# A transformer sandwich layer on one core: output projection three tiles ahead of the mixture, and a last tile in another order

## The chip, the cores and the metric

The kernel runs on one core of a Trainium2 chip. The metric is the device time of one execution, in microseconds (us). The core has five engines with a program each: TensorE (PE in the profile; its weight loads are PEld), VectorE (DVE), ScalarE (ACT), GpSimd (POOL) and SyncE (SP), which issues the DMAs here. Each executes in the order of its own program; they meet only at semaphores.

## The reference

```python
x = x + layernorm(attention(layernorm(x)))      # x: 4 x 512 x 1024, float32
x = x + layernorm(mixture(layernorm(x)))

def attention(x):   # 16 heads of 64, rotary on q and k, causal softmax
    ...
    return out @ Wo                              # Wo: 1024 x 1024

def mixture(x):     # 8 experts of rank 16
    scores = 8 * softmax(x @ Wr.T + br)
    low = einsum('bsd,hrd->bshr', x, A)
    return 2 * einsum('bshr,hor,bsh->bso', low, B, scores)
```

Every float32 product is made of three: each factor is split into a high and a low part, and high x high, low x high and high x low are added in PSUM.

## The kernel before, in words

The first part (projections, rotary, attention per pair of heads) writes the attention output to a scratch tensor and isn't touched. The part that matters here runs over 16 token tiles of 128 tokens. A tile t passes through these steps (names as in the code):

- `y_half`: y(t) = oT(t) @ Wo, on PE: 8 chunks by 3 products by two halves of 512 columns, 48 matmuls, into the two banks `y_ps[i]`, i = t % 2.
- `y_variance`, `ln_scale`: the layernorm's statistics on DVE (`bn_stats`, `bn_aggr`), the reciprocal root on ACT (Ln, Exp) refined on DVE; then ACT writes z in two halves; DVE adds the input (`x1`); statistics again and ACT writes `xn2`, the normalised tile.
- `x2_turn`, k = 0 and 1: PE transposes xn2, four blocks at a time, into the single bank `tr_ps`; ACT copies the high part (`x2T_high`), DVE subtracts the low part (`x2T_lo`). Because there is one bank, k = 1 waits until both have read k = 0.
- `low_rank`: 24 matmuls of 136 columns into `o_ps` give low and the router's logits; DVE and ACT make the softmax and the weighted low (`wlow`).
- one transpose of wlow (`wlt_done`), high and low part by ACT and DVE (`wlT_hi`, `wlT_lo`), and `experts`: 6 matmuls of 512 columns into `pt_ps`.
- a third layernorm (its number is `ln_third`), res on ACT, the last addition on POOL, the store by SP.

All engines walk through `turn(t, i)`, t = 0 to 17: in turn t, y is made for tile t, the middle steps (`x2_turn`, `low_rank`) for tile t - 1, and `experts`, the third layernorm and the store for tile t - 2. PE's turn puts the pieces of the other tiles between parts of y(t): first 15 matmuls of y(t), the transpose of wlow, 9 more, experts, 12 more, `x2_turn` k = 0, 9 more, `x2_turn` k = 1, the last 3, `low_rank`. y(0) is made in the last slots of attention. ACT's turn has x2T_high of the middle tile at its start and xn2(t) at its end. In turn 0, after xn2(0), ACT and DVE also split the mixture's constants (`ar`, `bt`, lines 759, 760, 1013, 1015). Nothing but these written orders and the semaphores sets what runs when.

## Time and profile before

| | |
|---|---|
| median of 3 runs | 1184.49 us (1184.37 to 1185.08) |
| profiled execution | 1184.45 us, span from first to last instruction 1182.7 us |
| PE busy | 1089.5 us, 92% of the span |
| DVE, ACT, POOL busy | 756.7, 628.3, 438.3 us |
| mean granted TensorE clock | 0.970 of full speed |

Times in the rows count from the start of the span. In a timeline row the first number is the start, the second the duration (of the matmuls the modelled one, which overlaps the next; the distance of two starts is what one costs), and the bracket is how long the engine was idle before it and what ended the wait. A row without a bracket follows its predecessor without a wait worth telling.

### The profile page before, as it was taken

The page shows a single profiled execution, that of the slowest core. Times are in us where ns is not written, and L with a number is a line of the kernel's source. Part 1 is how long each engine was busy: PE and PEld are TensorE (multiplying, and loading weights), DVE is VectorE, ACT ScalarE, POOL GpSimd, SP SyncE. Part 2 cuts the span into 40 slices and gives each one's busy share as a digit, 9 for nine tenths or more (in the row PEclk, how much of TensorE's full clock was granted, in tenths as well). Part 3 has the DMA queues.
Part 4 walks back from the last instruction along what each step waited for, and adds up shares of the span by engine and source line. Part 5 has one row for each costly group of instructions (what it writes and reads, how often), then busy time and mean ns, then how long its engine had stood idle before and what let it go on. Part 6 is the DMA issues. An engine that isn't in the chain of part 4 may idle for free.

```text
span 1182.7 us, 20255 instructions
## 1 busy us (share of the span) xinstructions
PE 1089.5 (92%) x5616; PEld 905.7 (77%) x5616; DVE 756.7 (64%) x2075; ACT 628.3 (53%) x1435; POOL 438.3 (37%) x412
## 2 busy tenths in 40 slices
PE   2899999999999776899999999999976999999984
PEld 2688888888888664688888888888865888888873
DVE  7656666666666675666666666666664666666663
ACT  4445555555555545555555555555564454544542
POOL 3053543535435232153543535435253223323311
PEclk9999999999999988999999999999989999999995
DMA  5111101111012113011101101010424132333210
GB/s 213 54 36 33 63 13 62 44 31 62 14 61 82 43 59 98 5 50 28 62 24 51 49 27 62 27 48 14 134 63 140 57 104 95 101 106 106 84 40 36
DMA packets 37499, 73.44 MB, mean 62 GB/s; under 512 B 3152, under 2 KB 19536, under 8 KB 37456
## 3 DMA queue, kind: packets, MB, share of 16 engines
q1 hardware_dynamic: 37456, 72.92, 19.0%
q8 instruction: 20, 0.33, 0.1%
q14 instruction: 23, 0.19, 0.1%
HBM read 56.14 MB, written 16.78 MB: 62 GB/s over the span
## 4 chain that ended last, share of the span: by engine, by line
PE 78%; DVE 8%; ACT 6%; issue 6%; DMA 1%; POOL 1%; POOLq 0%; DVEq 0%; SPq 0%; ACTq 0%
PE bank L1076 40%; PE bank L1034 30%; PE bank L1103 5%; ACT prob L591 1%; PE bank L1055 1%; PE bank L1195 1%; DVE prob L833 1%; DVE big_lo L822 1%; ACT pT_hi L602 1%; DVE q_hl L865 1%; DVE stats L776 1%; DVE stats L777 1%; DVE rr L797 1%; ACT xn L561 1%; DMA w_raw<-in_wqkv 1%
## 5 line engine op out<-in xcount | busy, mean ns | idle before, releaser
L1076 PE MATMUL bank<-big_hi,w_hi 128*128 128x512 f32 x768 | 335.9, 437 | 16.1 <-DVE big_lo L822 13.4
L474 POOL TENSOR_SCALAR prob<-prob,rinv 128x128 f32<-128x128 f32 (+3 forms) x256 | 156.6, 612 | 508.6 <-DVE rinv L843 508.6
L591 ACT ACTIVATE prob<-prob,nmax 128x128 f32<-128x128 f32 (+3 forms) x256 | 143.6, 561 | 353.4 <-DVE nmax L833 352.1
L1076 PE MATMUL bank<-big_hi,w_lo 128*128 128x512 f32 x768 | 306.4, 399 | 0.0
L1076 PE MATMUL bank<-big_lo,w_hi 128*128 128x512 f32 x768 | 304.4, 396 | 0.0
L1076 PEld LDWEIGHTS bank<-big_hi,w_hi 128*128 128x128 f32 x768 | 147.5, 192 | 33.7 <-issue 17.5
L1076 PEld LDWEIGHTS bank<-big_hi,w_lo 128*128 128x128 f32 x768 | 146.2, 190 | 34.4
L851 DVE TENSOR_TENSOR pT_lo<-bank,pT_hi 128x128 fp32r<-128x128 f32 (+3 forms) x256 | 123.9, 484 | 57.4 <-ACT pT_hi L602 54.1
L1076 PEld LDWEIGHTS bank<-big_lo,w_hi 128*128 128x128 f32 x768 | 148.4, 193 | 12.0
L843 DVE RECIPROCAL rinv<-rsum 128x1 f32<-128x1 f32 x256 | 40.8, 160 | 159.2 <-ACT prob L591 159.1
L833 DVE CUSTOM_DVE_ANT_0 prob<-bank,mask 128x128 f32<-128x128 f32 (+3 forms) x256 | 124.3, 486 | 22.3 <-PE bank L1034 18.4
L1103 PE MATMUL bank<-ident,prob 128*128 128x128 f32 x640 | 113.3, 275 | 1.5 <-DVE pT_lo L851 1.5
L1034 PE MATMUL bank<-big_hi,w_hi 128*128 128x512 f32 x256 | 106.7, 417 | 7.7 <-POOL big_lo L516 5.2
L602 ACT ACTIVATE pT_hi<-bank 128x128 fp32r<-128x128 f32 (+3 forms) x256 | 108.7, 425 | 4.1 <-PE bank L1103 2.5
L1103 PEld LDWEIGHTS bank<-ident,prob 128*128 128x128 f32 x640 | 84.1, 142 | 31.8 <-issue 2.5
L1034 PE MATMUL bank<-big_lo,w_hi 128*128 128x512 f32 x256 | 101.6, 397 | 0.0
L1034 PE MATMUL bank<-big_hi,w_lo 128*128 128x512 f32 x256 | 101.0, 395 | 0.0
L492 POOL TENSOR_TENSOR w_lo<-w_sum,w_hi 128x1024 fp32r<-128x1024 f32 x32 | 85.7, 2679 | 11.7 <-ACT w_hi L584 11.7
L1034 PE MATMUL bank<-k_hh,q_hl 128*128 128x128 f32 (+3 forms) x256 | 83.1, 325 | 2.4 <-DVE k_hh L872 1.9
L1034 PE MATMUL bank<-k_lo,q_hl 128*128 128x128 f32 (+3 forms) x256 | 83.6, 326 | 0.0
L532 POOL TENSOR_TENSOR res<-res,x 128x1024 f32<-128x1024 f32 x16 | 38.3, 2396 | 120.3 <-ACT res L561 120.3
L1034 PE MATMUL bank<-pT_hi,v_hl 128*128 128x512 f32 (+3 forms) x256 | 76.6, 311 | 1.5 <-ACT pT_hi L602 1.5
(106 smaller groups left out, 1921.4 us busy)
## 6 DMA issues: line engine op xcount, KB each, us to landing
w_raw<-in_wqkv SPq DMA_DIRECT2D x48, 512.0 KB, 3.6
attention_out<-o_sum SPq DMA_DIRECT2D x64, 128.0 KB, 2.3
xin<-attention_out SPq DMA_DIRECT2D x16, 512.0 KB, 4.8
xres<-in_x SPq DMA_DIRECT2D x16, 512.0 KB, 3.5
out<-res SPq DMA_DIRECT2D x16, 512.0 KB, 2.6
xin<-in_x SPq DMA_DIRECT2D x14, 512.0 KB, 3.7
w_raw<-in_wo SPq DMA_DIRECT2D x6, 512.0 KB, 4.3
prob<-in_x SPq DMA_DIRECT2D x2, 512.0 KB, 7.7
```

Of the source, the lines that this page charges most:

```text
L474: pool.tensor_scalar(p, p, rinv[:, q % 4:q % 4 + 1], 1.0, ALU.mult, ALU.mult).then_inc(prob_done, 1)
L492: pool.tensor_tensor(w_lo[:, m, :], src, w_hi[:, m, :].bitcast(F32), ALU.subtract).then_inc(w_lo_done[m], 1)
L532: pool.tensor_tensor(res[:, i, :], res[:, i, :], x1[:, i, :], ALU.add).then_inc(res_done, 1)
L561: return act.activation(dst, src, ACT.Identity, bias=nmr[:, 0:1], scale=rstd[:, 0:1])
L591: act.activation(prob[:, q % 4, 0:n], prob[:, q % 4, 0:n], ACT.Exp, scale=-1.0, bias=nmax[:, q % 4:q % 4 + 1], accum_out=rsum[:, q % 4:q % ...
L602: act.activation(pT_hi[:, h, 0:i + 1, P * i:P * i + P], pt_ps[q % 2][:, 0:P * (i + 1)].rearrange("p (j t) -> p j t", j=i + 1), ACT.Copy).t ...
L833: dve.tensor_tensor_reduce(prob[:, q % 4, 0:n], sc_ps[q % 2][:, 0:n], mask[:, SEQ - n:SEQ], -SOFT, 3e38, ALU.add, ALU.min, nmax[:, q % 4:q ...
L843: dve.reciprocal(rinv[:, q % 4:q % 4 + 1], rsum[:, q % 4:q % 4 + 1]).then_inc(inv_done, 1)
L851: dve.tensor_tensor(pT_lo[at], pt_ps[q % 2][:, 0:P * (i + 1)].rearrange("p (j t) -> p j t", j=i + 1), pT_hi[at].bitcast(F32), ALU.subtract ...
L1034: mm = pe.matmul(dst, lhsT, rhs, start=first and n == 0, stop=last and n == len(terms) - 1)
L1076: done = pe.matmul(grp_ps[(b + k) % 2][:, :], w, xt, start=at == 0, stop=at == GROUP_MM - 1)
L1103: last = pe.transpose(pt_ps[q % 2][:, P * j:P * j + P], prob[:, q % 4, P * j:P * j + P], ident[:, :])
```

## The change

Everything behind `y_half` moves one turn later: in turn t the middle steps belong to tile t - 2, and experts, third layernorm and store to tile t - 3, so there are 19 turns (0 to 18). x1 gets four buffers and xn2 two, since they live longer. The turns run through a common `run_turns`, whose loop covers four turns at a time (turns 4 to 11); the last seven are written out. The numbers of the layernorms follow the new order.

In turn 15 (`last`), y(15) is not divided by `x2_turn`: its second half runs whole, and both `x2_turn`s of tile 13 and low_rank(13) come behind it. ACT and DVE have an order of their own there. In turn 18 the last res goes in two halves: ACT signals each, DVE (not POOL) adds each, and SP stores each. out_out starts at 16 so that its counts fit.

```diff
-        x1 = sb(sC, "x1", [P, 2, EMBED])
+        x1 = sb(sC, "x1", [P, 4, EMBED])
-        xn2 = sb(sC, "xn2", [P, EMBED])
+        xn2 = sb(sC, "xn2", [P, 2, EMBED])
+        last_done = sem("last_done")
...
-            return TILES + 3 * t - 1 if late(t, 2) else TILES + 2 * t
+            return TILES + 3 * t - 2 if late(t, 2) else TILES + 2 * t
...
-            return 4 * TILES - 1 if isinstance(t, int) and t == TILES - 1 else TILES + 3 * t + 4
+            return 2 * TILES + TILES + t if isinstance(t, int) and t >= TILES - 3 else TILES + 3 * t + 6
+        def run_turns(eng, turn):
+            for t in range(4):
+                turn(t, t)
+            with eng.Fori(4, TILES - 7, 4) as t:
+                for j in range(4):
+                    turn(t + j, j)
+            for t in range(TILES - 4, TILES + 3):
+                turn(t, t % 4)
...
+                sp.sem_inc(out_out[h], 16)
...
-                if tiled(t - 2):
-                    sp.wait_ge(res_done, t - 1)
-                    sp.dma_start(out[bass.ds((t - 2) * P, P), :], res[:, i, :]).then_inc(out_out[i], 16)
+                if isinstance(t, int) and t == TILES + 2:
+                    for k in range(2):
+                        cols = slice(512 * k, 512 * k + 512)
+                        sp.wait_ge(last_done, k + 1)
+                        sp.dma_start(out[(TILES - 1) * P:TILES * P, cols], res[:, 1 - i, cols]).then_inc(out_out[1 - i], 16)
+                elif tiled(t - 3):
+                    sp.wait_ge(res_done, t - 2)
+                    sp.dma_start(out[bass.ds((t - 3) * P, P), :], res[:, 1 - i, :]).then_inc(out_out[1 - i], 16)
...
-                if tiled(t - 2):
-                    pool.wait_ge(normed, ln_third(t - 2) + 1)
-                    pool.tensor_tensor(res[:, i, :], res[:, i, :], x1[:, i, :], ALU.add).then_inc(res_done, 1)
+                if tiled(t - 3) and not (isinstance(t, int) and t == TILES + 2):
+                    pool.wait_ge(normed, ln_third(t - 3) + 1)
+                    pool.tensor_tensor(res[:, 1 - i, :], res[:, 1 - i, :], x1[:, (j + 1) % 4, :], ALU.add).then_inc(res_done, 1)
...
-            def turn(t, i):
-                if tiled(t - 2):
-                    ln_start(ln_third(t - 2))
-                middle = tiled(t - 1) and not (isinstance(t, int) and t > TILES)
-                if middle:
-                    x2T_high(t - 1, 0)
-                if tiled(t - 2):
-                    act.wait_ge(ln_dve, LN_STEPS * (ln_third(t - 2) + 1))
+            def turn(t, j):
+                i = j % 2
+                middle = tiled(t - 2) and not (isinstance(t, int) and t > TILES + 1)
+                last = isinstance(t, int) and t == TILES - 1
+                if tiled(t - 3):
+                    ln_start(ln_third(t - 3))
+                if middle and not last:
+                    x2T_high(t - 2, 0)
+                if tiled(t - 3):
+                    act.wait_ge(ln_dve, LN_STEPS * (ln_third(t - 3) + 1))
                     if late(t, 4):
-                        act.wait_ge(out_out[i], 8 * (t - i) - 16)
-                    for k in range(2):
-                        done = normal(res[:, i, 512 * k:512 * k + 512], pt_ps[k][:, :])
-                    done.then_inc(normed, 1)
-                if middle:
-                    x2T_high(t - 1, 1)
+                        act.wait_ge(out_out[1 - i], 8 * (t - 3 - (1 - i)) + 16)
+                    if isinstance(t, int) and t == TILES + 2:
+                        for k in range(2):
+                            normal(res[:, 1 - i, 512 * k:512 * k + 512], pt_ps[k][:, :]).then_inc(normed, 1)
+                    else:
+                        for k in range(2):
+                            done = normal(res[:, 1 - i, 512 * k:512 * k + 512], pt_ps[k][:, :])
+                        done.then_inc(normed, 1)
+                if middle and not last:
+                    x2T_high(t - 2, 1)
                 if tiled(t) and late(t, 1):
                     ln_start(ln_first(t))
-                if middle:
-                    act.wait_ge(soft_dve, 5 * (t - 1) + 2)
+                if last:
+                    x2T_high(t - 2, 0)
+                if middle and not last:
+                    act.wait_ge(soft_dve, 5 * (t - 2) + 2)
                     act.activation(lexp[:, :], logit[:, :], ACT.Exp, bias=lmax[:, 0:1],
                                    accum_out=lsum[:, 0:1]).then_inc(soft_exp, 1)
                 if tiled(t):
...
                     for k in range(2):
                         done = normal(z[:, 512 * k:512 * k + 512], y_ps[i][k][:, :])
                     done.then_inc(normed, 1)
+                if last:
+                    x2T_high(t - 2, 1)
+                    act.wait_ge(soft_dve, 5 * (t - 2) + 2)
+                    act.activation(lexp[:, :], logit[:, :], ACT.Exp, bias=lmax[:, 0:1],
+                                   accum_out=lsum[:, 0:1]).then_inc(soft_exp, 1)
                 if tiled(t + 2) and not (isinstance(t, int) and t >= TILES - 2):
                     oT_high(t + 2, i, 8 * (t + 2 - i) + 16)
-                if middle:
-                    act.wait_ge(wlt_done, t)
-                    if late(t, 2):
-                        act.wait_ge(e_done, t - 1)
-                    act.activation(wlT_hi[:, :], o_ps[:, WLT:WLT + P], ACT.Copy).then_inc(wlT_hi_done, 1)
+                if middle and not last:
+                    wlT_high(t)
                 if tiled(t):
                     ln_rstd(ln_second(t))
-                    normal(xn2[:, :], x1[:, i, :]).then_inc(normed, 1)
+                    normal(xn2[:, i, :], x1[:, j, :]).then_inc(normed, 1)
+                if last:
+                    wlT_high(t)
                 if isinstance(t, int) and t == 0:
                     act.wait_ge(ffn_in, 48)
                     act.activation(ar_hi[:, :, :], ar_raw[:, :, :], ACT.Copy).then_inc(ffn_hi_done, 1)
                     act.activation(bt_hi[:, :], bt_raw[:, :], ACT.Copy).then_inc(ffn_hi_done, 1)
+            def wlT_high(t):
+                act.wait_ge(wlt_done, t - 1)
+                if late(t, 3):
+                    act.wait_ge(e_done, t - 2)
+                act.activation(wlT_hi[:, :], o_ps[:, WLT:WLT + P], ACT.Copy).then_inc(wlT_hi_done, 1)
+            run_turns(act, turn)
...
+            def turn(t, j):
+                i = j % 2
+                middle = tiled(t - 2) and not (isinstance(t, int) and t > TILES + 1)
+                if tiled(t - 3):
+                    dve.wait_ge(e_done, t - 2)
+                    layernorm(ln_third(t - 3), [e[:, :] for e in pt_ps])
+                if isinstance(t, int) and t == TILES + 2:
+                    for k in range(2):
+                        cols = slice(512 * k, 512 * k + 512)
+                        dve.wait_ge(normed, ln_third(TILES - 1) + 1 + k)
+                        dve.tensor_tensor(res[:, 1 - i, cols], res[:, 1 - i, cols], x1[:, (j + 1) % 4, cols], ALU.add
+                                          ).then_inc(last_done, 1)
+                if isinstance(t, int) and t == TILES - 1:
+                    y_variance(t, i)
+                    ln_scale(ln_first(t))
+                    x2T_low(t - 2, 0)
+                    residual(t, j)
+                    x2T_low(t - 2, 1)
+                    soft_max(t - 2)
+                    residual_norm(t, j)
+                    soft_scale(t - 2)
+                    wlT_low(t - 2)
+                    return
                 if middle:
+                    x2T_low(t - 2, 0)
+                    x2T_low(t - 2, 1)
...
-            def turn(t, i):
+            def turn(t, j):
+                i = j % 2
                 running = tiled(t) and not (isinstance(t, int) and t == 0)
-                middle = tiled(t - 1) and not (isinstance(t, int) and t > TILES)
+                middle = tiled(t - 2) and not (isinstance(t, int) and t > TILES + 1)
+                last = isinstance(t, int) and t == TILES - 1
                 if running:
                     y_half(t, i, 0, 0, 5)
-                if tiled(t - 2):
-                    pe.wait_ge(wlow_done, t - 1)
+                if tiled(t - 3):
+                    pe.wait_ge(wlow_done, t - 2)
                     pe.transpose(o_ps[:, WLT:WLT + P], wlow[:, :], ident[:, :]).then_inc(wlt_done, 1)
                 if running:
                     y_half(t, i, 0, 5, KC)
-                if tiled(t - 2):
-                    experts(t - 2)
+                if tiled(t - 3):
+                    experts(t - 3)
                 if running:
-                    y_half(t, i, 1, 0, 4)
+                    y_half(t, i, 1, 0, KC if last else 4)
                 if middle:
-                    x2_turn(t - 1, 0)
-                if running:
+                    x2_turn(t - 2, i, 0)
+                if running and not last:
                     y_half(t, i, 1, 4, 7)
                 if middle:
-                    x2_turn(t - 1, 1)
-                if running:
+                    x2_turn(t - 2, i, 1)
+                if running and not last:
                     y_half(t, i, 1, 7, KC)
                 if middle:
-                    low_rank(t - 1)
+                    low_rank(t - 2)
+            run_turns(pe, turn)
```

Two places show how the instructions move. On ACT, the end of turn 0 and turn 1 of the kernel before (xn is xn2, w_hi holds oT's high part):

```order
L561 ACTIVATE xn<-x,nmr,rstd 128x1024 [waits ln_dve]
L759 ACTIVATE ar_hi<-ar_raw 128x1088 [waits ffn_in]
L760 ACTIVATE bt_hi<-bt_raw 128x1024
L710 ACTIVATE x2T_hi<-bank 128x512 [waits x2t_done] x2
L552 ACTIVATE lnv<-ve 128x1 [waits ln_dve]
L554 ACTIVATE r<-lnv 128x1 [waits ln_act]
L734 ACTIVATE lexp,lsum<-logit,lmax 128x8 [waits soft_dve]
L561 ACTIVATE z<-bank,nmr,rstd 128x512 [waits ln_dve]
L561 ACTIVATE z<-bank,nmr,rstd 128x512
L691 ACTIVATE w_hi<-xin 128x1024 [waits y_done,oT_in1]
```

and from the same instruction in the changed kernel:

```order
L566 ACTIVATE xn<-x,nmr,rstd 128x1024 [waits ln_dve]
L775 ACTIVATE ar_hi<-ar_raw 128x1088 [waits ffn_in]
L776 ACTIVATE bt_hi<-bt_raw 128x1024
L557 ACTIVATE lnv<-ve 128x1 [waits ln_dve]
L559 ACTIVATE r<-lnv 128x1 [waits ln_act]
L566 ACTIVATE z<-bank,nmr,rstd 128x512 [waits ln_dve]
L566 ACTIVATE z<-bank,nmr,rstd 128x512
L696 ACTIVATE w_hi<-xin 128x1024 [waits y_done,oT_in1]
L557 ACTIVATE lnv<-ve 128x1 [waits ln_dve]
L559 ACTIVATE r<-lnv 128x1 [waits ln_act]
L566 ACTIVATE xn<-x,nmr,rstd 128x1024 [waits ln_dve]
L715 ACTIVATE x2T_hi<-bank 128x512 [waits x2t_done] x2
```

The x2T_hi copies of tile 0 stood directly behind the constants; now they stand behind z, the copy of oT and xn2 of tile 1.

On DVE, the kernel before from the softmax of tile 14 to the statistics of tile 15 (turn 15):

```order
L974 TENSOR_TENSOR logit<-bank,br_sb 128x8 [waits low_done]
L976 TENSOR_REDUCE lmax<-logit 128x1 [waits soft_dve]
L797 SCALAR_TENSOR_TENSOR rr<-r,ve 128x1 [waits ln_dve,ln_act]
L800 TENSOR_SCALAR cc<-rr 128x1 [waits ln_dve]
L804 TENSOR_TENSOR rstd<-cc,r 128x1 [waits ln_dve,normed]
L806 SCALAR_TENSOR_TENSOR nmr<-mv,rstd 128x1 [waits ln_dve]
L981 RECIPROCAL linv<-lsum 128x1 [waits soft_exp]
L983 TENSOR_SCALAR score<-lexp,linv 128x8 [waits soft_dve]
L988 TENSOR_TENSOR wlow<-bank,score 128x128 [waits wlt_done,soft_dve]
L1003 TENSOR_TENSOR x<-z,xres 128x1024 [waits res_done,xres_in1,normed]
L1006 TENSOR_TENSOR wlT_lo<-bank,wlT_hi 128x128 [waits wlT_hi_done]
L776 BN_STATS stats<-x 128x6 [waits x1_done]
```

and in the changed kernel, turn 15 from the addition that makes x1(15):

```order
L1011 TENSOR_TENSOR x<-z,xres 128x1024 [waits res_done,xres_in1,normed]
L973 TENSOR_TENSOR x2T_lo<-bank,x2T_hi 128x512 [waits x2T_hi_done]
L978 TENSOR_TENSOR logit<-bank,br_sb 128x8 [waits low_done]
L980 TENSOR_REDUCE lmax<-logit 128x1 [waits soft_dve]
L791 BN_STATS stats<-x 128x6 [waits x1_done]
L792 BN_STATS stats<-x 128x6
L802 BN_AGGR mv<-stats 128x2 [waits ln_stat]
L804 TENSOR_SCALAR ve<-mv 128x1 [waits ln_stat]
L812 SCALAR_TENSOR_TENSOR rr<-r,ve 128x1 [waits ln_dve,ln_act]
L815 TENSOR_SCALAR cc<-rr 128x1 [waits ln_dve]
L819 TENSOR_TENSOR rstd<-cc,r 128x1 [waits ln_dve,normed]
L821 SCALAR_TENSOR_TENSOR nmr<-mv,rstd 128x1 [waits ln_dve]
```

The statistics of x1(15) stood right behind x1 and one small subtraction; now the second x2T_lo and the two softmax operations of tile 13, which wait for low_rank(13), stand between, and the softmax's second part stands behind the whole layernorm.

## Rows read from the trace of the kernel before

**Rows 1.** PE timeline at the start: start us, us, engine line op out<-in count [idle <-releaser]

```profile
902.40 0.47 PE L1034 MATMUL bank<-big_hi,w_hi 128*128 128x512 f32 x1 [1.45 <-issue]
...
910.41 0.39 PE L1034 MATMUL bank<-big_lo,w_hi 128*128 128x512 f32 x1
915.18 1.12 PE L1195 MATMUL bank<-ident,xn 128*128 128x128 f32 x4 [4.38 <-ACT xn L561]
...
924.17 0.44 PE L1034 MATMUL bank<-big_hi,w_hi 128*128 128x512 f32 x1
```

**Rows 2.** PE timeline: first matmul of y(3) and y(15), a transpose, last of y(15)

```profile
940.24 0.44 PE L1034 MATMUL bank<-big_hi,w_hi 128*128 128x512 f32 x1
...
1133.06 0.44 PE L1034 MATMUL bank<-big_hi,w_hi 128*128 128x512 f32 x1
...
1142.87 0.60 PE L1195 MATMUL bank<-ident,xn 128*128 128x128 f32 x4
...
1146.27 0.39 PE L1034 MATMUL bank<-big_lo,w_hi 128*128 128x512 f32 x1
```

**Rows 3.** ACT timeline at the start: xn2 of tile 0

```profile
913.89 1.24 ACT L561 ACTIVATE xn<-x,nmr,rstd 128x1024 f32<-128x1024 f32 x1 [0.94 <-DVE nmr L806]
```

**Rows 4.** DVE timeline at the start: x1 of tile 0, last of the constants

```profile
909.40 1.23 DVE L1003 TENSOR_TENSOR x<-z,xres 128x1024 f32<-128x1024 f32 x1 [6.32 <-DMA xres<-in_x]
...
918.31 1.22 DVE L1015 TENSOR_TENSOR bt_lo<-bt_raw,bt_hi 128x1024 fp32r<-128x1024 f32 x1
```

**Rows 5.** DMA issues on the page: out<-in, count, KB each, median us to landing

```profile
attention_out<-o_sum SPq DMA_DIRECT2D x64, 128.0 KB, 2.3
...
out<-res SPq DMA_DIRECT2D x16, 512.0 KB, 2.6
```

**Rows 6.** Windows: stretch, length, busy by engine, then granted PE clock, DMA share, GB/s

```profile
910.00:916.00 6.00, 1.62 (x9) 1.16 (x7) 2.96 (x9) 2.52 (x4) 0.00 (x0) 0.81 0.72 265
916.00:920.00 4.00, 4.00 (x11) 2.74 (x9) 2.90 (x3) 1.55 (x3) 0.00 (x0) 0.50 0.00 0
920.00:924.00 4.00, 3.86 (x31) 3.62 (x31) 2.27 (x6) 0.60 (x1) 0.00 (x0) 0.94 0.00 0
1157.00:1166.60 9.60, 7.22 (x32) 6.65 (x32) 3.16 (x10) 3.85 (x7) 2.36 (x1) 0.50 0.14 56
```

**Rows 7.** PE timeline at the end: experts(14), transposes, low_rank(15), experts(15)

```profile
1153.52 0.76 PE L1034 MATMUL bank<-bt_hi,wlT_hi 128*128 128x512 f32 x1 [1.92 <-issue]
...
1160.47 1.09 PE L1195 MATMUL bank<-ident,xn 128*128 128x128 f32 x4 [1.51 <-DVE x2T_lo L964]
1161.21 0.46 PE L1034 MATMUL bank<-ar_hi,x2T_hi 128*128 128x136 f32 x1
...
1166.16 0.41 PE L1034 MATMUL bank<-ar_lo,x2T_hi 128*128 128x136 f32 x1
...
1169.53 0.76 PE L1034 MATMUL bank<-bt_hi,wlT_hi 128*128 128x512 f32 x1 [0.74 <-ACT wlT_hi L752]
```

**Rows 8.** DVE timeline at the end

```profile
1147.25 0.69 DVE L776 BATCH_NORM_STATS2 stats<-bank 128x6 f32<-128x512 f32 x1
...
1166.61 0.17 DVE L974 TENSOR_TENSOR logit<-bank,br_sb 128x8 f32<-128x8 f32 x1 [3.70 <-PE bank L1034]
...
1172.47 0.70 DVE L776 BATCH_NORM_STATS2 stats<-bank 128x6 f32<-128x512 f32 x1 [3.04 <-PE bank L1034]
```

**Rows 9.** ACT timeline at the end

```profile
1156.56 1.24 ACT L561 ACTIVATE xn<-x,nmr,rstd 128x1024 f32<-128x1024 f32 x1 [0.93 <-DVE nmr L806]
...
1159.00 0.60 ACT L710 ACTIVATE x2T_hi<-bank 128x512 fp32r<-128x512 f32 x1 [0.24 <-PE bank L1195]
...
1175.71 1.45 ACT L561 ACTIVATE res<-bank,nmr,rstd 128x512 f32<-128x512 f32 x2 [0.94 <-DVE nmr L806]
```

**Rows 10.** POOL and SP timelines at the end: last addition, issue of the last store

```profile
1177.23 2.34 POOL L532 TENSOR_TENSOR res<-res,x 128x1024 f32<-128x1024 f32 x1 [13.65 <-ACT res L561]
...
1179.60 0.33 SPq L440 DMA_DIRECT2D out<-res  x1
```

More of the change, by code:

```diff
@@ L760, in turn @@
                     act.activation(bt_hi[:, :], bt_raw[:, :], ACT.Copy).then_inc(ffn_hi_done, 1)
-            turn(0, 0)
-            turn(1, 1)
-            turn(2, 0)
-            turn(3, 1)
-            with act.Fori(4, TILES - 2, 2) as t:
-                turn(t, 0)
-                turn(t + 1, 1)
-            for t in range(TILES - 2, TILES + 2):
-                turn(t, t % 2)
+            def wlT_high(t):
[4 more added lines that the diff above has]
+            run_turns(act, turn)
         @block.vector
@@ L953, in _, with x2T_low @@
             run_slots(dve, slot)
[L956 to L967 removed]
+            def x2T_low(t, k):
+                dve.wait_ge(x2T_hi_done, 2 * t + k + 1)
+                dve.tensor_tensor(x2T_lo[:, 4 * k:4 * k + 4, :], tr_ps[:, :].rearrange("p (c t) -> p c t", c=4),
+                                  x2T_hi[:, 4 * k:4 * k + 4, :].bitcast(F32), ALU.subtract).then_inc(x2T_lo_done, 1)
@@ new lines, in wlT_low, with residual @@
+            def wlT_low(t):
+                dve.wait_ge(wlT_hi_done, t + 1)
+                dve.tensor_tensor(wlT_lo[:, :], o_ps[:, WLT:WLT + P], wlT_hi[:, :].bitcast(F32), ALU.subtract
+                                  ).then_inc(wlT_lo_done, 1)
+            def residual(t, j):
+                dve.wait_ge(normed, ln_first(t) + 1)
+                dve.wait_ge(xres_in[j % 2], 8 * (t - j % 2) + 16)
+                if late(t, 4):
+                    dve.wait_ge(res_done, t - 3)
+                if isinstance(t, int) and t == 0:
+                    dve.wait_ge(pv_done, HEADS * BATCHES)
+                    for h in range(2):
+                        dve.wait_ge(o_out[h], 16 * UNITS)
+                dve.tensor_tensor(x1[:, j, :], z[:, :], xres[:, j % 2, :], ALU.add).then_inc(x1_done, 1)
@@ L970, in turn @@
                 if middle:
[L972 to L976 removed]
+                    soft_max(t - 2)
                 if tiled(t):
@@ L1016, in turn @@
                                       ).then_inc(ffn_lo_done, 1)
-            turn(0, 0)
-            turn(1, 1)
-            turn(2, 0)
-            turn(3, 1)
-            with dve.Fori(4, TILES - 2, 2) as t:
-                turn(t, 0)
-                turn(t + 1, 1)
-            for t in range(TILES - 2, TILES + 2):
-                turn(t, t % 2)
+            run_turns(dve, turn)
         @block.tensor
@@ L1185, in _, with x2_turn @@
             pe.wait_ge(osum_done, HEADS * BATCHES)
-            def x2_turn(t, k):
+            def x2_turn(t, i, k):
                 if k == 0:
@@ L1194, in x2_turn @@
                 for c in range(4):
-                    last = pe.transpose(tr_ps[:, P * c:P * c + P], xn2[:, P * (4 * k + c):P * (4 * k + c) + P],
+                    last = pe.transpose(tr_ps[:, P * c:P * c + P], xn2[:, i, P * (4 * k + c):P * (4 * k + c) + P],
                                         ident[:, :])
```

104 lines of the change are left out of this document (33 added, 71 removed).

## The prediction, on record before the changed kernel ran

> **What bounds the kernel now.** I read the PE timeline of the second part first, then the timelines of DVE and ACT at its two ends, and last the windows with the granted clock. In the middle PE has no idle time: the first matmul of y(3) starts at 940.24 and that of y(15) at 1133.06 [rows 2], 192.82 us for 12 turns, 16.07 us each, and the transposes at 1142.87 follow without a wait. Every turn before and after the change holds the same PE instructions, so the middle can't give or take much. What can change is the time up to y(3) and the time behind y(15).
>
> At the start PE runs 36 matmuls of y(1) from 902.40 to 910.41 (0.229 us from start to start), then sits for 4.38 us until xn2(0) is written, and works at half clock after it [rows 1, 3]: the granted clock is 0.81 over 910 to 916, 0.50 over 916 to 920 and 0.94 over 920 to 924 [rows 6]. At the end, y(15) is done at 1146.27 + 0.39 = 1146.66 [rows 2], and the span ends 36.04 us later at 1182.7. This tail is a chain of latencies, PE at half clock (0.50 over 1157 to 1166.6 [rows 6]).
>
> **The start.** What the change is to remove is the wait for xn2(0) inside y(1). Since turn 1 has no middle steps now, y(1) runs whole: 902.40 + 48 x 0.229 = 913.4, and y(2) follows; its oT is ready (ACT copies the high part of oT(2) ahead of xn2(0), which starts at 913.89 [rows 3], and POOL has nothing else to do than the low part). After 36 matmuls, at 921.6, come the transposes of tile 0, k = 0, whose input is written since 915.13 [rows 3], then 9 matmuls to 924.1. Now k = 1 needs x2T_hi(0,0) and x2T_lo(0,0). On ACT this copy no longer stands behind the constants but behind xn2 of tile 1. That comes like this:
> - DVE is busy with the constants until 918.31 + 1.22 = 919.5 [rows 4], and only then takes the statistics of y(1), although y(1) is done at 913.6.
> - One layernorm, from the first statistics to ACT's scaled copy, takes 1175.71 - 1172.47 = 3.24 us [rows 8, 9]. So z(1) starts at 922.7 and, with 1.45 for its halves [rows 9], ends at 924.2.
> - From the start of an x1 addition to the end of xn2 it took 913.89 + 1.24 - 909.40 = 5.73 [rows 3, 4], so xn2(1) ends at 929.9.
> - From the start of an x2T_hi copy to PE's k = 1 transposes it took 1160.47 - 1159.00 = 1.47 [rows 7, 9]: 931.3.
>
> PE thus waits from 924.1 to 931.3, 7.2 us in place of 4.38. After that its clock is at half, as it was after the shorter wait before. From 931.3: transposes to the next matmul 0.74 (1161.21 - 1160.47 [rows 7]), the last 3 matmuls of y(2) at half clock 6 x 0.229 = 1.4, so low_rank(0) starts at 933.4. Its 24 matmuls take 5.36 at half clock (1161.21 to 1166.16 + 0.41 [rows 7]) and half of that at full. Before, the clock came back about 5 us after PE restarted (915.18 to about 920 [rows 1, 6]); with the same here, at 936.2, 13 of them run slow (2.8) and 11 fast (1.2), and y(3) starts at 937.4. Bounds: 935.0 with all of it at full clock, 938.6 with all of it slow. Before it was 940.24: y(3) is 2.8 us earlier (1.6 to 5.2).
>
> That is not all gain: by 940.24 PE had also done experts(0), x2_turn(1) and low_rank(1), which the changed kernel still owes, one turn of it, at the end.
>
> **The middle.** Twelve turns of 16.07 us each. The new requirement, x2T_high(t-2) behind xn2(t-1) on ACT, comes in the same place of the turn as xn2(t-1) itself did for the transposes, which had no wait [rows 2]. The later consumers get more room; buffers: x1 and xn2 have more of them, the others are reused at the same distance. The res_done and out_out waits look one store back as before. Cost 0 (bounds: 0 to one ACT copy of 0.60 [rows 9] per turn, 7.2 in all; none of the rows shows that it fails, so I take 0). y(15) starts at 937.4 + 192.8 = 1130.2.
>
> **The last tile unbroken.** y(15) took 1146.66 - 1133.06 = 13.60 with two groups of transposes inside. Without them, each about two matmul slots of 0.229 (the modelled duration is 0.60 [rows 2]), 12.7. So y(15) is done at Y = 1142.9, 3.7 us before the old 1146.66; 0.9 of that comes from this edit, but the transposes are only moved behind it.
>
> **The tail, counted from Y.** Left for PE: x2_turn(13), low_rank(13), experts(13), the same for 14 and for 15. Before, only the second half of the work for 14 and all for 15 stood there.
> - Up to experts(13). DVE takes the statistics of y(15) at once (before, it had an x2T_lo first and started 1147.25 - 1146.66 = 0.59 late [rows 8]). z starts at 3.27, ends at 4.7, x1(15) is done at 6.0. The k = 0 transposes run at once, but x2T_lo(13,0) stands on DVE behind the layernorm's scale: 3.24 + 0.69, and PE's k = 1 starts at 4.1. By then PE has been idle for 3.5 us and its clock is at half. low_rank(13): 4.1 + 0.74 = 4.8 to 10.2. The softmax's two operations of DVE wait for it, and behind them stand the statistics of x1(15), ready at 6.0: this is a wait that the change adds, 4.6 us. They start at 10.6, xn2(15) starts at 13.8, ends at 15.1. The rest of the softmax of tile 13 stands behind this layernorm on DVE, and the copy wlT_hi(13) behind xn2(15) on ACT. So wlow(13) at 14.7, wlT_hi at 15.4, wlT_lo at 15.7, experts(13) at 15.9. (With full clock in low_rank(13): 13.9.)
> - Two cycles. From experts(n) through the transposes of the next tile, low_rank, softmax and wlow to experts(n+1) it took 1169.53 - 1153.52 = 16.01 us [rows 7]. In between, ACT's copy waits for the third layernorm's statistics, DVE's subtraction for its scale, k = 1 for both: the same order in turns 16 and 17 now. Before there was one such cycle, now there are two, 13 to 14 and 14 to 15: 32.0.
> - From experts(15) to the end it took 1182.7 - 1169.53 = 13.17 [rows 7]. POOL's addition of 2.34 [rows 10] becomes two DVE additions, of which the second counts: half of 1.23 [rows 4], 0.6. The store is issued in halves, the first long before. A store of 512 KB lands 2.6 after its issue and one of 128 KB 2.3 [rows 5], so the landing gives 0 to 0.3, and SP's issue takes 0.33 [rows 10] as before. I take 1.7 off: 11.5.
>
> Sum: 15.9 + 32.0 + 11.5 = 59.4, where it was 36.0. The span ends at 1142.9 + 59.4 = 1202.3. The profiled execution lasted 1184.45 with a span of 1182.7, 1.75 more, and it agrees with the median of 1184.49. So 1204.0, 19.5 us above before: -3.7 for y(15), +23.3 for the tail.
>
> The Trainium skill's page "DMA: Bandwidth & Descriptors" (Anatomy of one DMA) gives a transfer a fixed part of about 2 us and a part by its bytes; by it the half store would land some 0.6 us sooner, where the rows here give at most 0.3. No term uses it.
>
> **Rivals.**
> 1. The clock is full where I have it at half. For it speaks that the tail now holds more PE work; against it that low_rank(15) with the transposes ahead of it, 1160.47 to 1166.57 without a gap, ran at 0.50 throughout [rows 6, 7]. It gives: start 2.4, experts(13) 2.0, and per cycle low_rank with its k = 1 transposes 2.5, experts 1.3, the transpose of wlow 0.2, together 4.0; experts(15) 1.3. 2.4 + 2.0 + 8.0 + 1.3 = 13.7: 1190. The skill's "TensorE: Matmul & The Clock Gate" (What's actually happening) says that the clock is low by default and that activity releases it; this rule speaks for this rival, and the trace's 6 us of low_rank(15) speak against it here.
> 2. The copy x2T_hi(0,0) doesn't hold PE at the start, and the gap closes as intended: y(2) from 913.4 with 48 matmuls, 8 transposes (0.9) and low_rank(0) (2.7) leads to 928.0 for y(3), 9.4 before my 937.4: 1194.6. Against it stands ACT's written order.
> 3. The other side, faster than before: the work of tiles 13 and 14 fits below tile 15's own chain. Then the tail is the old 36.04 less 0.59 less 1.7, and the end is 1142.9 + 33.8 + 1.75 = 1178.4. It decides at Y + 15.1, when xn2(15) is there: experts(14) would have to be done by then. At full clock PE needs only about 10 us for all of it (8 matmul slots of 0.23 for transposes, 48 of 0.11, 12 of 0.23), which speaks for it; against it speaks that DVE and ACT put tile 13's softmax and wlT_hi behind the layernorm of tile 15, so that not even experts(13) starts before 15.1.
> 4. The middle loses up to 0.60 per turn: 1211.
>
> **How the numbers follow.** Forecast 1204.0 with chance 0.79; rival 1 0.06, rival 2 0.05, rival 3 0.05, rival 4 0.05. The forecast's own range is the start's bounds (-2.4, +1.2), the clock in low_rank(13) (-2.0), the store in halves giving nothing (+1.7) and less than a microsecond over several hand-overs: 1198 to 1208, which leaves out the rivals, 2 in 10. A change under 0.2% (2.4 us) is what a measurement can't tell from none. Faster 0.05 (rival 3), the same 0.01, slower 0.94.
>
> **What would show it.** In the profile after: no PE wait at 910.8, but one of about 7 us from 924 to 931 that ends with x2T_lo behind ACT's x2T_hi; turns of 16.07 us; y(15) done near 1143; a DVE wait for low_rank(13) ahead of the statistics of x1(15); three groups of experts in the tail, 16 us apart; the last addition on DVE, 0.6 each. Wrong would be a tail with experts(13) ahead of xn2(15), a clock above 0.9 in it, or y(3) starting before 935 or after 939.

## The result, and the profile after

The changed kernel took 1204.51 us, median of 4 runs (1203.41 to 1208.78), the kernel before 1184.57 (1184.37 to 1185.08) on the same chip: a ratio of 1.0174 (95% interval 1.0149 to 1.0200). It is slower, by 20 us, and the forecast was 1204.0. The profiled execution lasted 1203.73 with a span of 1201.8.

All times below are read from a span's start. The attention part ahead of this one is untouched, but it ends up to 3.3 us sooner or later from run to run. So "aligned" means: counted from the start of x1(0), the first addition of this part on DVE, which stands at 909.40 before [rows 4] and at 907.74 after, and put on the clock of the kernel before. Before the changed place is reached, after is 1.66 us ahead for no reason of its own. The distance from the first matmul of y(1) to x1(0) itself differs among the profiles, 6.73 to 7.58 us (7.00 before), so an aligned time is good to some half a microsecond.

**The start.** PE's timeline of the changed kernel: first matmul of y(1), the transposes behind the 84 matmuls of y(1) and of y(2) up to there, the wait, low_rank(0), y(3), y(4), y(15).

```profile
901.01 0.47 PE L1072 MATMUL bank<-big_hi,w_hi 128*128 128x512 f32 x1 [1.45 <-issue]
...
920.18 0.60 PE L1233 MATMUL bank<-ident,xn 128*128 128x128 f32 x4
...
929.61 1.08 PE L1233 MATMUL bank<-ident,xn 128*128 128x128 f32 x4 [6.77 <-DVE x2T_lo L973]
...
931.78 0.32 PE L1072 MATMUL bank<-ar_hi,x2T_hi 128*128 128x136 f32 x1
...
936.80 0.73 PE L1072 MATMUL bank<-big_hi,w_hi 128*128 128x512 f32 x1
...
953.91 0.44 PE L1072 MATMUL bank<-big_hi,w_hi 128*128 128x512 f32 x1
...
1130.65 0.44 PE L1072 MATMUL bank<-big_hi,w_hi 128*128 128x512 f32 x1
```

The wait of 4.38 us for xn2(0) inside y(1) [rows 1] is gone and one of 6.77 stands at 922.85. What released it is on ACT's timeline and then DVE's: the copy x2T_hi(0,0) runs only behind z(1), the copy of oT and xn2(1), and these hang on DVE's statistics of y(1), which start when the constants are done.

```profile
912.23 1.25 ACT L566 ACTIVATE xn<-x,nmr,rstd 128x1024 f32<-128x1024 f32 x1 [0.94 <-DVE nmr L821]
...
921.05 1.45 ACT L566 ACTIVATE z<-bank,nmr,rstd 128x512 f32<-128x512 f32 x2 [0.94 <-DVE nmr L821]
...
927.02 1.24 ACT L566 ACTIVATE xn<-x,nmr,rstd 128x1024 f32<-128x1024 f32 x1 [0.94 <-DVE nmr L821]
928.17 0.58 ACT L715 ACTIVATE x2T_hi<-bank 128x512 fp32r<-128x512 f32 x1
```

```profile
916.67 1.22 DVE L1061 TENSOR_TENSOR bt_lo<-bt_raw,bt_hi 128x1024 fp32r<-128x1024 f32 x1
917.80 0.69 DVE L791 BATCH_NORM_STATS2 stats<-bank 128x6 f32<-128x512 f32 x1
...
928.77 0.69 DVE L973 TENSOR_TENSOR x2T_lo<-bank,x2T_hi 128x512 fp32r<-128x512 f32 x1 [1.79 <-ACT x2T_hi L715]
```

The windows (stretch, length, busy time of PE, PEld, DVE, ACT, POOL, then the granted clock, DMA share and GB/s):

```profile
901.00:921.00 20.00, 19.98 (x90) 16.59 (x91) 8.76 (x23) 6.40 (x10) 2.39 (x1) 1.00 0.41 141
921.00:931.00 10.00, 3.23 (x15) 2.48 (x14) 4.27 (x11) 4.79 (x8) 2.44 (x1) 0.72 0.34 105
931.00:936.00 5.00, 5.00 (x24) 4.81 (x22) 2.31 (x5) 0.74 (x3) 0.00 (x0) 0.50 0.01 3
936.00:940.00 4.00, 4.00 (x15) 3.35 (x15) 1.84 (x10) 2.16 (x5) 0.00 (x0) 0.62 0.00 0
1143.00:1147.00 4.00, 0.78 (x6) 0.45 (x4) 2.77 (x9) 1.27 (x4) 2.19 (x1) 1.00 0.24 97
1147.00:1153.00 6.00, 5.67 (x27) 5.70 (x28) 2.01 (x3) 1.67 (x3) 0.00 (x0) 0.52 0.06 23
1158.00:1175.00 17.00, 10.64 (x41) 8.94 (x40) 5.24 (x17) 4.10 (x11) 2.37 (x1) 0.50 0.08 31
1175.00:1191.00 16.00, 10.09 (x40) 8.74 (x40) 4.95 (x16) 3.61 (x9) 2.37 (x1) 0.61 0.09 34
```

PE restarts at 929.61, works at half clock over 931 to 936, and even the first matmuls of y(3) are slow (0.62 over 936 to 940). y(3) starts at 936.80, aligned 938.46, against 940.24 before [rows 2]. Turn 3 takes 17.11 us (953.91 - 936.80) because of its slow beginning, and the eleven turns from there 16.07 each, as before ((1130.65 - 953.91) / 11).

**The tail.** PE's timeline from the last matmul of y(15) on: the transposes of tile 13 and low_rank(13), the transpose of wlow(13), and the first matmul of experts(13), (14), (15).

```profile
1142.95 0.39 PE L1072 MATMUL bank<-big_lo,w_hi 128*128 128x512 f32 x1
1143.18 0.60 PE L1233 MATMUL bank<-ident,xn 128*128 128x128 f32 x4
1147.33 1.08 PE L1233 MATMUL bank<-ident,xn 128*128 128x128 f32 x4 [3.56 <-DVE x2T_lo L973]
...
1157.73 0.48 PE L1271 MATMUL bank<-ident,wlow 128*128 128x128 f32 x1 [4.30 <-DVE wlow L991]
1158.95 0.77 PE L1072 MATMUL bank<-bt_hi,wlT_hi 128*128 128x512 f32 x1 [0.74 <-ACT wlT_hi L783]
...
1174.91 0.77 PE L1072 MATMUL bank<-bt_hi,wlT_hi 128*128 128x512 f32 x1 [0.74 <-ACT wlT_hi L783]
...
1190.87 0.77 PE L1072 MATMUL bank<-bt_hi,wlT_hi 128*128 128x512 f32 x1 [0.74 <-ACT wlT_hi L783]
```

y(15) ends at 1143.34 (before 1146.66), but three groups of experts lie behind it where two did [rows 7], 15.96 us apart. Between y(15) and experts(13) lies the order of DVE: x1(15) is added from 1148.10, and its statistics wait behind the softmax of tile 13.

```profile
1148.10 1.23 DVE L1011 TENSOR_TENSOR x<-z,xres 128x1024 f32<-128x1024 f32 x1 [0.91 <-ACT z L566]
1149.24 0.68 DVE L973 TENSOR_TENSOR x2T_lo<-bank,x2T_hi 128x512 fp32r<-128x512 f32 x1
1153.47 0.17 DVE L978 TENSOR_TENSOR logit<-bank,br_sb 128x8 f32<-128x8 f32 x1 [3.55 <-PE bank L1072]
...
1153.76 0.68 DVE L791 BATCH_NORM_STATS2 stats<-x 128x6 f32<-128x512 f32 x1
...
1193.81 0.70 DVE L791 BATCH_NORM_STATS2 stats<-bank 128x6 f32<-128x512 f32 x1 [3.04 <-PE bank L1072]
...
1197.86 1.36 DVE L1027 TENSOR_TENSOR res<-res,x 128x512 f32<-128x512 f32 x2 [0.85 <-ACT res L566]
```

In the last line are the two halves of the last addition, where POOL's one took 2.34 [rows 10]. From experts(15) to the end: 1201.8 - 1190.87 = 10.93, before 13.17. The view of waits over the tail (1143 to 1202) adds them up: total, times, longest. Each hand-over of the chain stands there three times, once for each tile (while DVE waits for the logits PE works, in the other two PE waits):

```profile
DVE logit L978 <- PE bank L1072: 10.9, 3, 3.7
PE bank L1233 <- DVE x2T_lo L973: 10.1, 3, 3.6
...
PE bank L1271 <- DVE wlow L991: 7.8, 3, 4.3
```

### The profile page after: what moved, and what is told of

The parts are those of the page before. It is cut to its first block, busy times and chain, and to the rows that moved or that the text cites. A ratio compares the mean times of both kernels' runs of the same rounds, so it can differ in the third digit from the quotient of the medians.

```text
span 1201.8 us, 20121 instructions
## 1 busy us (share of the span) xinstructions
PE 1100.6 (92%) x5616; PEld 916.4 (76%) x5616; DVE 758.7 (63%) x2077; ACT 628.1 (52%) x1435; POOL 435.8 (36%) x411
## 4 chain that ended last, share of the span: by engine, by line
PE 76%; DVE 10%; ACT 7%; issue 5%; DMA 1%; POOL 1%; DVEq 0%; ACTq 0%; SPq 0%
PE bank L1114 38%; PE bank L1072 30%; PE bank L1141 5%; ACT prob L596 1%; PE bank L1233 1%; PE bank L1093 1%; DVE prob L848 1%; DVE stats L791 1%; DVE q_hl L880 1%; DVE stats L792 1%; DVE big_lo L837 1%; ACT pT_hi L607 1%; ACT k_hh L622 1%; DVE rr L812 1%; ACT o_low L640 1%
## 5 line engine op out<-in xcount | busy, mean ns | idle before, releaser
L1114 PE MATMUL bank<-big_hi,w_hi 128*128 128x512 f32 x768 | 336.0, 438 | 16.1 <-DVE big_lo L837 13.4
```

The source lines that it names most:

```text
L1114: done = pe.matmul(grp_ps[(b + k) % 2][:, :], w, xt, start=at == 0, stop=at == GROUP_MM - 1)
```

## The experiments

The first four undo or alter one part of the changed kernel each, and are compared with it by their spans. Their ratios are to the kernel before.

**The last addition whole again** (the third layernorm's copy, the addition on POOL and the store of tile 15 as before; the first condition stands in SP's, ACT's and DVE's turn, the second in POOL's).

```diff
-                if isinstance(t, int) and t == TILES + 2:
+                if False:
...
-                if tiled(t - 3) and not (isinstance(t, int) and t == TILES + 2):
+                if tiled(t - 3):
```

> The changed kernel with the last tile's addition whole on POOL and its store whole again. Theory (latency chain at the end): from the start of experts(15) to the end it took 13.17 us before and 10.93 after, so 2.2 us come back and it is slower than the changed kernel: 1206 us. Rival (the halves are hidden or the stores' fixed time eats them): 1204 us, no difference.

Measured: 1207.4 us (1205.6 to 1210.18), 1.0187 (1.0163 to 1.0212), span 1203.8. Experts(15) starts at 1190.60, the end is 13.2 later and not 10.93. The halves are a gain of 2.3 us. In the medians the surplus over the kernel before beside it is 21.6 us here and 19.9 with the halves.

**The last tile with an ordinary turn** (y(15) broken by the transposes of tile 13, and low_rank(13) directly behind it; `last` on ACT and PE, and DVE's own order of turn 15).

```diff
-                last = isinstance(t, int) and t == TILES - 1
+                last = False
...
-                if isinstance(t, int) and t == TILES - 1:
+                if False:
```

> The changed kernel with turn 15 in the ordinary order (y(15) broken by the transposes of tile 13, tile 13's softmax and wlT ahead of tile 15's layernorm). Theory: experts(13) starts about 6.9 us behind the end of y(15), as experts(14) did before, instead of 15.6, and y(15) ends 0.9 later, so 7.8 us less: about 1196 us; still one more cycle of 16 us in the tail than before. Rival 1 (what counts is the end of y(15)): 0.9 us slower than the changed kernel, 1205. Rival 2 (the whole loss comes from the last tile's order): 1184 or less.

Measured: 1195.74 us (1192.27 to 1199.78), 1.0085 (1.0056 to 1.0114), span 1193.4. PE's timeline there, the transposes inside and behind y(15), then the one of wlow(13) and experts(13):

```profile
1140.38 0.60 PE L1233 MATMUL bank<-ident,xn 128*128 128x128 f32 x4
1142.89 0.60 PE L1233 MATMUL bank<-ident,xn 128*128 128x128 f32 x4
1148.80 0.33 PE L1271 MATMUL bank<-ident,wlow 128*128 128x128 f32 x1 [2.00 <-DVE wlow L991]
1151.04 0.76 PE L1072 MATMUL bank<-bt_hi,wlT_hi 128*128 128x512 f32 x1 [1.92 <-issue]
```

y(15) ends 0.8 us later (1144.17), experts(13) starts 7.9 us sooner, and with a section that starts at the same time (x1(0) 907.81 and 907.74) the span is 8.4 us shorter. Of the faults that these four runs undo, leaving the last tile unbroken is thus the dearest: it takes the transposes from within y(15), where other matmuls cover their waits and they cost 0.9 us, and puts them and low_rank(13) behind it, where each step waits for another engine and PE is at half clock.

**The copies of tile 0 in time** (x2T_hi(0,0) and (0,1) on ACT and x2T_lo on DVE in turn 1 and no longer in turn 2, ahead of xn2(1) on ACT and behind x1(1) on DVE).

```diff
+                if isinstance(t, int) and t == 1:
+                    x2T_high(0, 0)
+                    x2T_high(0, 1)
...
+                if isinstance(t, int) and t == 1:
+                    x2T_low(0, 0)
+                    x2T_low(0, 1)
```

> The changed kernel with the two x2T_hi and x2T_lo copies of tile 0 moved from the start of turn 2 into turn 1, between x1(1) and its layernorm. Theory: PE's wait of 6.8 us in y(2) shrinks to about 2 us, the clock stays full, and y(3) starts at about 928.4 instead of 936.8, with 1.0 us more saved in y(3) at full clock: 9.4 us less, about 1195 us. Rival (the middle is bound by the ACT and DVE chain, so an earlier y(3) is lost again, or xn2(1), now later, holds turn 3): 1200 to 1204.

Measured: 1200.06 us (1198.32 to 1204.83), 1.0131 (1.0102 to 1.0160), span 1196.4, aligned 7.0 us shorter than that of the changed kernel (x1(0) at 909.30), against 9.4 expected. PE's timeline and the windows there:

```profile
926.35 0.87 PE L1240 MATMUL bank<-ident,xn 128*128 128x128 f32 x4 [2.38 <-DVE x2T_lo L977]
...
928.30 0.32 PE L1079 MATMUL bank<-ar_hi,x2T_hi 128*128 128x136 f32 x1
...
931.75 0.45 PE L1079 MATMUL bank<-big_hi,w_hi 128*128 128x512 f32 x1
```

```profile
924.00:926.00 2.00, 0.00 (x0) 0.00 (x0) 1.71 (x2) 1.48 (x3) 0.93 (x1) 1.00 0.00 0
926.00:931.00 5.00, 4.65 (x25) 4.39 (x25) 2.64 (x7) 1.00 (x3) 1.52 (x1) 0.66 0.69 210
```

The cause of the wait was right: with the copies moved it falls from 6.77 to 2.38 us. I had expected the clock to stay full across so short a wait. It didn't: it was at half for 3.7 us behind the restart, which costs 1.8, and y(3) starts 1.8 us later than expected. The rest of the missing 2.4 lies in turn 3, which took 16.77 us and not 16.07, with short waits in it (0.18 for wlow(0)).

**Tile 15's layernorm ahead of tile 13's softmax** in the last turn: on DVE as shown, on ACT the exponential behind xn2(15) in the same way.

```diff
                     x2T_low(t - 2, 1)
-                    soft_max(t - 2)
                     residual_norm(t, j)
+                    soft_max(t - 2)
```

> The changed kernel with tile 15's layernorm ahead of tile 13's softmax on DVE and ACT in turn 15. Theory: the wait of the statistics of x1(15) for low_rank(13) goes (3.6 us), xn2(15) is written about 4 us earlier, but experts(13) only gains some 1.9 us because wlow(13) then waits for low_rank(13) and the softmax: 1202 us. Rival 1 (that wait is wholly on the path): 3.6 us less, 1200. Rival 2 (xn2(15) has slack and experts(13) is held by something else): 1204, no change.

Measured: 1202.04 us (1200.57 to 1208.54), 1.0153 (1.0118 to 1.0187), span 1198.6, 3.2 below the changed kernel's. xn2(15) starts at 1152.98 in place of 1156.98, experts(13) 13.4 us behind y(15) in place of 15.6: 2.2 us for the wait that the change put ahead of the statistics. The rest is a first cycle of 15.12 instead of 15.96, in which the clock was fuller (0.61 over 1156 to 1172, where the changed kernel has 0.50 over 1158 to 1175).

**The broken last tile and the early copies together** (all that was found against the change, undone, with one tile further ahead kept).

> The changed kernel with the ordinary turn 15 and the early copies of tile 0 together, the best that is left of running three tiles ahead. Theory: the two add up (8.4 and 7.0 us of span in their profiles), span 1186.4, about 1188 us: still some 4 us above before, since the tail holds one more cycle of 16 us. Rival (three ahead pays once its two faults are mended): below 1184.

Measured: 1191.25 us (1189.49 to 1196.19), 1.0056 (1.0034 to 1.0078). y(15) ends at 1141.53, aligned 1141.5 and 5.2 us ahead of the kernel before; but the span is 7.6 us longer. It is a miss by 3 us: expected were 1188. The difference lies in the start. PE waited only 1.97 us there, and yet its clock was 0.50 over 928 to 937: low_rank(0) and the first twelve matmuls of y(3) ran slow, turn 3 took 18.48 us (951.19 - 932.71), and y(4) starts 2.5 us later, aligned, than in the third experiment. PE's restart and the first matmul of y(3):

```profile
926.49 0.63 PE L1240 MATMUL bank<-ident,xn 128*128 128x128 f32 x4 [1.97 <-DVE x2T_lo L977]
...
932.71 0.73 PE L1079 MATMUL bank<-big_hi,w_hi 128*128 128x512 f32 x1
```

PE's first matmuls of experts(13), (14), (15):

```profile
1148.40 0.76 PE L1079 MATMUL bank<-bt_hi,wlT_hi 128*128 128x512 f32 x1 [1.78 <-issue]
...
1163.46 0.77 PE L1079 MATMUL bank<-bt_hi,wlT_hi 128*128 128x512 f32 x1 [0.74 <-ACT wlT_hi L787]
...
1179.41 0.77 PE L1079 MATMUL bank<-bt_hi,wlT_hi 128*128 128x512 f32 x1 [0.74 <-ACT wlT_hi L787]
```

Before, experts(14) stood 6.86 us behind y(15) (1153.52 - 1146.66); here experts(13) stands there (6.87), and one more serial cycle of 15 to 16 us follows. That is what the tile further ahead costs by itself, and it is more than the 5.2 us that this start gives back.

The next five put single parts on the kernel before.

**Only the halves, on the kernel before.**

> The kernel before with only the last edit of the change: the last res signalled in halves, added in halves by DVE and stored in halves. Theory: the same 2.2 us as between the changed kernel and its whole variant, so 0.998 of before, 1182.3 us; in the profile, experts(15) to the end 10.9 instead of 13.2 us. Rival: no difference, 1184.5.

Measured: 1182.07 us (1180.91 to 1185.4, 10 runs), 0.9979 (0.9968 to 0.9990). Experts(15) at 1167.60, the end at 1178.5, 10.9 later, not 13.17. The fifth kernel above has the halves too and differs from this one by the tile further ahead and the order at its start; beside the same kernel before it took 1191.25 us. That is 9.2 us more, the net price of the distance.

**The halves, and PE's idle time in the tail filled** with matmuls that write a bank nobody reads any more (the first of them wait until z(14) is written): 7, 7, 11 and 8 of them ahead of wlow's transpose, experts(14) and the two transposes of tile 15, then 7 and 2 ahead of the last transpose and experts(15).

```diff
+            def fill(n):
+                for _ in range(n):
+                    pe.matmul(y_ps[0][0][:, :], oT_hi[:, 0, 0, :], wo_hi[:, 0, 0:512], start=True, stop=True)
...
+                if end:
+                    fill(7)
                 if tiled(t - 2):
                     pe.wait_ge(wlow_done, t - 1)
```

> The kernel before with the halves and with extra matmuls that nothing reads, put on PE into its waits behind y(15): 7, 7, 11, 8 in turn 16 (ahead of the transpose of wlow(14), of experts(14), of the first and of the second transposes of tile 15) and 7 and 2 in turn 17. They write a bank that is free. Theory: PE's clock stays full, low_rank(15) takes 2.8 instead of 5.4 us, experts(15) 1.5 instead of 2.9: some 4.2 us less than with the halves alone, 1178. Rival 1 (the clock falls all the same, the fillers only delay what stands behind them): 1182 to 1186. Rival 2 (the tail is bound by DVE and ACT and doesn't care for the clock): 1182.

Measured: 1177.93 us (1176.39 to 1179.29), 0.9940 (0.9922 to 0.9959). The windows of its tail:

```profile
1150.00:1157.00 7.00, 6.38 (x28) 4.64 (x28) 4.95 (x18) 2.70 (x9) 0.00 (x0) 1.00 0.13 50
1157.00:1166.00 9.00, 8.54 (x53) 7.00 (x52) 4.35 (x16) 4.51 (x9) 2.37 (x1) 1.00 0.09 37
```

The clock stays full where it was 0.50 before [rows 6]. Experts(15) follows experts(14) by 13.34 us (1167.63 - 1154.29) in place of 16.01 and takes 1.6 in place of 2.9. Beyond the halves that is 4.1 us of the aligned span: what a full clock gives in this tail with these fillers in it.

**The start rewritten, the distance as before** (PE's turn 1 below): y(1) whole, then y(2) with the transposes of tile 0 in it and low_rank(0) behind 3/4 of it; ACT's and DVE's turn 1 in an order of their own, the constants between the steps.

```diff
+                if isinstance(t, int) and t == 1:
+                    y_half(1, 1, 0, 0, KC)
+                    y_half(1, 1, 1, 0, KC)
+                    y_half(2, 0, 0, 0, 4)
+                    x2_turn(0, 0)
+                    y_half(2, 0, 0, 4, KC)
+                    x2_turn(0, 1)
+                    y_half(2, 0, 1, 0, 4)
+                    low_rank(0)
+                    return
```

> The kernel before (still two tiles ahead) with only its start rewritten: y(1) whole, the transposes and low_rank of tile 0 between pieces of y(2), the layernorm of y(1) ahead of the splitting of the constants on DVE and ACT, and the third layernorm of tile 0 behind the x2T copies of tile 1. Theory: PE's wait of 4.4 us and its half clock go, y(3) starts at about 934.3 instead of 940.2, the tail stays: 5.9 us less, 1178.6. Rival (the work of the constants and of tile 0 only waits in another place, in turn 2 or 3): 1182 to 1186.

Measured: 1182.77 us (1180.85 to 1184.69, 10 runs), 0.9982 (0.9970 to 0.9993). A miss: y(3) starts at 931.80, aligned 933.7 as expected, but 15 matmuls on PE waits 3.31 us for wlow(1), since the softmax of tile 1 stands on DVE behind the third layernorm of tile 0 and the statistics of y(2). Within that order one small DVE operation took 1.68 us in place of 0.22 (last section), which is 1.5 of the 3.3. Aligned, 1.7 us are left of 5.9.

**The same with that order mended** (the layernorm of y(2) first, the softmax of tile 1 between the halves of the third layernorm of tile 0, x1(2) in a buffer of its own).

> The rewritten start of b3_start, and in turn 2 the layernorm of y(2) now stands ahead of the third layernorm of tile 0, with the softmax of tile 1 inside the latter, and x1 of tile 2 has a buffer of its own so that it needn't wait for POOL's addition of tile 0. Theory: in b3_start PE waited 3.3 us in y(3) for wlow(1) and fell to half clock; without it turn 3 passes in about 16.5 us and y(4) starts some 4 us earlier: 4 us less than b3_start, 1178.5. Rival (another link of the same chain is as late, exp(1) or xn2(2)): no less than b3_start, 1182 to 1183.

Measured: 1180.3 us (1179.52 to 1185.52), 0.9974 (0.9958 to 0.9989). Aligned span 4.4 us shorter than before: no wait for wlow(1), a last one of 0.89 at the transposes of tile 2. It is a miss too, expected were 1178.5. In the medians the gain is 3.2 us, that of the first rewritten start was 2.0, and their intervals overlap: that the mended order is the better one is read from the profiles, not from the times.

**All together, on the kernel before**: this start, the halves and the filled tail.

> b5_start2 with the halves and the extra matmuls of b2_fill. Theory: start and tail don't touch each other, so 6 us (start) and 6.8 us (tail) add up: 1172, ratio 0.989. Rival (the gains overlap): 1176 to 1178.

Measured: 1173.67 us (1172.2 to 1175.87), 0.9912 (0.9895 to 0.9929), the fastest kernel of this study. Its aligned span is 10.8 us shorter, which is 4.4 for the start and 6.4 for the tail: the parts add up, since they touch different ends.

## Why the prediction was right, by its steps

- **The start's wait.** Predicted 924.1 to 931.3, held by x2T_hi(0,0) behind xn2(1). Measured, aligned: 924.5 to 931.3. The third experiment moved the copies and the wait fell to 2.4.
- **The clock behind it.** The step "before, the clock came back about 5 us after PE restarted; with the same here" was wrong: it came back some 9 us after the restart at 929.61, and all of low_rank(0) and the first of y(3) ran slow. y(3) started at aligned 938.5 and not 937.4 (the upper bound was 938.6), and turn 3 was 1.0 us longer, which no bound of mine held. Together 2.1 us.
- **The middle.** Turns of 16.07, nothing lost behind turn 3. Right.
- **y(15) unbroken.** 12.69 us (1143.34 - 1130.65), predicted 12.7. Y stands at 1143.34, predicted 1142.9, but only because the section started 1.66 us early: aligned it is 1145.0, 2.1 too late, which is the clock's term.
- **Up to experts(13).** Y + 15.6, predicted 15.9. The added wait, statistics of x1(15) behind the logits of tile 13, was 4.4 us, predicted 4.6. What this order costs at experts(13) is 2.2, as the fourth experiment showed; the prediction gave no price for it alone.
- **Two cycles.** 15.96 each, predicted 16.01.
- **The end.** 10.93, predicted 11.5: the halves give 2.24 and not 1.7. The addition was sized right. It ends 0.72 us behind ACT's copy (1197.86 + 1.36 against 1197.05 + 1.45), before it was 2.41 (1177.23 + 2.34 against 1175.71 + 1.45 [rows 9, 10]): 1.69. The term that was mis-sized is the landing, for which I took 0 and allowed 0.3: from the end of the addition to the end of the span it takes 2.58 us with the half store and 3.13 with the whole one, 0.55 less. The page of the profile has it too, in the landings of the whole and the half stores of the changed kernel:

```profile
out<-res SPq DMA_DIRECT2D x15, 512.0 KB, 2.7
...
out<-res SPq DMA_DIRECT2D x2, 256.0 KB, 2.1
```

  The 128 KB row that the prediction took for a bound is of another transfer (attention_out, 2.3), and lands later than these 256 KB. The Trainium skill's "DMA: Bandwidth & Descriptors" (Anatomy of one DMA) had given 0.6, an estimate from the bytes. Its figures there are for DMAs that GpSimd issues, these stores are issued by SP; the 0.55 measured comes near them all the same.
- **The sum.** The tail was 58.46 us, predicted 59.4. The forecast hit within half a microsecond because three errors cancel: -1.66 for the earlier start of the section, +2.1 for the clock, -0.9 in the tail. On its own merits it was 1.2 us too low (2.1 - 0.9).

Rival 1 (full clock in the tail) fell on the trace: 0.50 to 0.61 over both cycles. Its price up to experts(13), 2.0, and with it the same term of the range, doesn't follow from the prediction's own lengths: low_rank at full clock is 2.7 us shorter and the transposes ahead of it 0.4, so 3.1; nothing in the forecast hangs on it. Its 4.0 per cycle is not shown: the filled tail gave 2.7. There DVE takes the statistics of experts(14) only behind the layernorm of x1(15), so shorter experts can't help; in the changed kernel DVE waits 3.04 us for PE at that place, and they might. Rival 2 fell on the wait of 6.77. Rival 4 fell on the turns of 16.07. Rival 3 fell as it was reasoned: experts(13) starts at 1158.95, behind the start of xn2(15) at 1156.98 and its end at 1158.22. The fourth experiment shows that it isn't only that order: with tile 15's layernorm first, the work of tiles 13 and 14 still doesn't fit beneath it.

So the change loses because what it shortens by running a tile further ahead (y(3) earlier by 1.8 us aligned, 8.4 with the copies in time) is less than the serial cycle of 16 us that the tile of distance adds behind the last y, and because the unbroken last tile adds 8.4 us to that. Only the halves gain. Not tried was the fifth kernel with a filled tail. By what the filling gave (a cycle of 13.34, where the fifth kernel has 15.06 and 15.95, and 1.3 in the last experts), I estimate 1185.6 for it (1191.25 - 1.72 - 2.61 - 1.3), about the time of the kernel before and still 7.7 us behind the same filling at the old distance.

## What to carry to other kernels

In a pipeline over few tiles like this one, a tile that one stage runs further ahead of the next is paid at the end by one cycle through all engines without cover (16 us here); count that cycle in the trace of the existing tail and compare it with the wait that the distance would remove. Work that waits for other engines belongs beneath the last long stretch of matmuls, not behind it, and the wait at the start is often an order on ACT or DVE that can be mended with the distance kept. Where the tail is a chain of latencies, TensorE's clock can be part of its length: here, keeping PE busy there gave 4 us.
